# Twelve-head attention of a small vision tower: values kept token-major and passed through DRAM instead of being spread and transposed

## The reference, cut to what matters

```python
qkv = x @ qkv_w.T + qkv_b
q, k, v = (qkv[0], qkv[1], qkv[2])          # B, heads, 17, 16
attn = softmax(einsum('bhqd,bhkd->bhqk', q, k) * scale, axis=-1)
out = einsum('bhqk,bhkd->bhqd', attn, v)
return out @ proj_w.T + proj_b
```

## Time and profile before

| | us |
|---|---|
| median of 3 runs | 935.1 |
| profiled execution, its own time | 934.2 |
| its span | 932.1 |
| stages a0, a2, a3 together | 299.9 |
| PE busy | 854.9 (92% of the span) |
| DVE busy | 447.4 (48%) |
| ACT busy | 387.8 (42%) |
| POOL busy | 186.7 (20%) |

### The profile page before, as it was taken

One profiled execution on the slowest core, in us unless ns is written; L12 is line 12 of the kernel. 1 busy time (PEld: TensorE's weight loads), 2 busy tenths in 40 slices (PEclk: granted clock), 3 DMA queues, 4 the chain that ended last, 5 costly groups with the idle time before them and its releaser, 6 DMA issues. The chain is left out here.

```text
span 932.1 us, 16890 instructions
## 1 busy us (share of the span) xinstructions
PE 854.9 (92%) x6194; PEld 608.5 (65%) x6195; DVE 447.4 (48%) x903; ACT 387.8 (42%) x857; POOL 186.7 (20%) x207
## 2 busy tenths in 40 slices
PE   6899888999998799999989789999999999999997
PEld 5556656677775467777668466765687566666776
DVE  5566676777744412222268666551104566633111
ACT  2366653453542022333243864554151455532332
POOL 0610003444500134445200012220000000002232
PEclk9999999999988899999999999999999999997999
DMA  8000000000004967112150019000000211102111
GB/s 294 1 2 1 1 2 0 1 2 1 1 2 102 256 182 198 46 51 46 39 164 3 0 45 258 6 2 28 1 1 1 56 50 50 52 19 97 43 51 34
DMA packets 30638, 51.07 MB, mean 55 GB/s; under 512 B 3750, under 2 KB 23752, under 8 KB 30572
## 3 DMA queue, kind: packets, MB, share of 16 engines
q1 hardware_dynamic: 22140, 36.09, 14.0%
q0 software_dynamic: 4416, 9.84, 3.8%
q10 hardware_dynamic: 4016, 4.23, 1.4%
HBM read 43.30 MB, written 6.83 MB: 54 GB/s over the span
## 5 line engine op out<-in xcount | busy, mean ns | idle before, releaser
L79 PE MATMUL banks<-con 128*128 128x512 f32 (+1 forms) x206 | 95.1, 572 | 3.0 <-DVEq L2136 1.4
L1846 PE MATMUL banks<-moe_wu,moe_xf 96*128 x256 | 92.1, 505 | 1.6 <-ACT moe_xf L1954 0.8
L634 PE MATMUL banks<-x,a_wqkv 96*96 96x272 f32 x288 | 74.6, 397 | 0.9 <-PEq L457 0.5
L1846 PEld LDWEIGHTS banks<-moe_wu,moe_xf 96*128 96x128 f32 x256 | 47.5, 195 | 31.4 <-issue 4.8
L944 ACT ACTIVATE a_vt<-banks 102x384 f32<-102x384 f32 x96 | 41.9, 488 | 50.4 <-PE banks L710 50.1
L154 ACT ACTIVATE ln_sq<-x 96x544 f32<-96x544 f32 x32 | 21.1, 658 | 93.2 <-DVE x L146 93.2
L634 PEld LDWEIGHTS banks<-x,a_wqkv 96*96 96x96 f32 x288 | 45.4, 164 | 18.2 <-issue 3.2
L79 PEld LDWEIGHTS banks<-con 128*128 128x128 f32 x206 | 38.4, 202 | 25.9 <-issue 22.4
L2151 DVE TENSOR_TENSOR moe_hid<-banks,moe_gs 128x384 f32<-128x384 f32 x32 | 17.9, 558 | 77.6 <-PE banks L1846 77.6
L710 PE MATMUL banks<-con,a_vx 96*102 96x96 f32 x384 | 42.7, 253 | 7.4 <-ACT a_vt L944 6.1
L2008 POOL DMA_INDIRECT moe_xs<-moe_x_rows,moe_taken x32 | 31.2, 974 | 76.1 <-PE banks L1830 54.2
(11 more groups left out here) (409 smaller groups left out, 1772.2 us busy)
## 6 DMA issues: line engine op xcount, KB each, us to landing
moe_wu<-in_moe_up SPq DMA_DIRECT2D x16, 576.0 KB, 8.9
f_w<-in_f_e SPq DMA_DIRECT2D x10, 576.0 KB, 14.6
moe_wd<-in_moe_down SPq DMA_DIRECT2D x16, 288.0 KB, 9.9
patch_px<-in_patches SPq DMA_DIRECT2D x4, 768.0 KB, 9.4
f_wu<-in_f_up SPq DMA_DIRECT2D x4, 582.0 KB
f_wd<-in_f_down SPq DMA_DIRECT2D x4, 576.0 KB
f_x_rows<-f_xtok ACTq DMA_DIRECT2D x4, 384.0 KB, 3.4
a_wqkv<-in_a_wqkv SPq DMA_DIRECT2D x3, 432.0 KB, 8.3
```

The costliest lines, as they stand in the source:

```text
L79: self.nc.tensor.matmul(self.ps[bank][:, 0:width], self.ident, self.con[:, 0:width], start=True, stop=True)
L634: last = nc.tensor.matmul(ps[2 + m][0:HD, 0:CW], wqkv[:, a, j * D + m * HD:j * D + (m + 1) * HD], chunk(x, c)[:, a], start=a == 0, stop=a ...
L1846: last = nc.tensor.matmul(ps[2 + 2 * p + u][:, 0:BW], xf[0:KU[a], p, a], wu[0:KU[a], bass.ds(e, 1), a, u * BW:(u + 1) * BW].rearrange("p e ...
```

## The change

The values are projected token-major: the tokens of `x` are the stationary operand and the value weights the moving one, so that a product gives [128 tokens, 192 features] in PSUM. `values(c)` makes eight such products per chunk (two blocks of 128 tokens and one of 32 for the last 16). ACT moves them to `vtok` in two instructions. SP writes them to a DRAM tensor `v_rows` (two planes of 272 rows of 96 features) with 4 DMAs per chunk, waits for these, and reads them back with 6 DMAs per chunk, one per head of a plane, into `vt`, now with (key, head) in the partitions. Each read writes 18 partitions x 32 pieces of 16 floats (64 bytes); the 18th is a row that no product uses and that makes the number even. `vt` and `vtok` hold two chunks: the read of chunk c waits until `weigh` is done with chunk c-2. Keys, scores and weights change their inner order from (head, key) to (key, head). The loads ahead are issued in four parts, part c after the read of chunk c+1. `spread_values`, `turn_values` and the old `take_values` are gone. In a3 the transposes of the inputs stay, under the name `turn_inputs`. POOL zeroes `vt` first (two memsets).

```diff
@@ ClassWeights
+    PARTS = ((0, 1), (2, 3), (4,), (5,))
...
@@ ExpertWeights
+    def load_part(self, sp, part):
+        self.load(sp, range(part, part + 1))
...
@@ stage_narrow_attention
-        vx = sb("vx", [HD, 2, 2, IC, HH * N])
-        vt = sb("vt", [HH * N, 2, GI, 2, HD])
+        vtok = sb("vtok", [128, 2, 2 * D + HD])
+        vt_rows = sb("vt", [(N + 1) * HH, 2, 2 * IC, HD])
+        vt = vt_rows[0:N * HH].rearrange("p c (a i) d -> p c a i d", a=2)
...
+        v_rows = nc.dram_tensor(name + "_v_rows", (NC, 2 * CW + 1, HD), F32).ap()
...
@@ block.sync
-            for w in ahead:
-                w.load(sp)
+            def write_values(c):
+                rows = v_rows[c, 0:2 * CW].rearrange("(a t) d -> t a d", a=2)
+                for u in range(2):
+                    sp.wait_ge(v_taken, 2 * c + 1)
+                    sp.dma_start(rows[128 * u:128 * (u + 1)], vtok[:, c % 2, u * D:(u + 1) * D].rearrange("p (a d) -> p a d", a=2)).then_inc(v_written, 16)
+                for a in range(2):
+                    sp.wait_ge(v_taken, 2 * c + 2)
+                    sp.dma_start(rows[256:CW, a], vtok[SLOT * (a + 1) - (CW - 256):SLOT * (a + 1), c % 2, 2 * D:2 * D + HD]).then_inc(v_written, 16)
+
+            def read_values(c):
+                sp.wait_ge(v_written, 64 * (c + 1))
+                if c < 2:
+                    sp.wait_ge(vt_zero, c + 1)
+                else:
+                    sp.wait_ge(ctx_ready, GPC * (c - 1))
+                for h in range(HH):
+                    sp.dma_start(vt_rows[h::HH, c % 2, :, h * HW:(h + 1) * HW],
+                                 bass.AP(v_rows.tensor, c * (2 * CW + 1) * HD + h * HW, [[HD, N + 1], [N * HD, 2 * IC], [1, HW]])).then_inc(v_in[c % 2], 16)
+
+            sp.wait_ge(vt_zero, 1)
+            sp.dma_start(v_rows[:, 2 * CW:2 * CW + 1].rearrange("c t d -> t c d"), vt_rows[0:1, 0, 0:NC]).then_inc(v_padded, 16)
+            write_values(0)
+            sp.wait_ge(v_padded, 16)
+            read_values(0)
+            for c in range(NC):
+                if c + 1 < NC:
+                    write_values(c + 1)
+                    read_values(c + 1)
+                for w in ahead:
+                    w.load_part(sp, c)
...
@@ block.tensor
+            def values(c):
+                if c in carried:
+                    pe.wait_ge(before.ready, c + 1)
+                if c >= 1:
+                    pe.wait_ge(v_taken, 2 * c)
+                for u in range(2):
+                    for a in range(2):
+                        tokens = chunk(x, c)[:, a, 128 * u:128 * (u + 1)]
+                        nc.tensor.matmul(v_bank[:, u * D:(u + 1) * D], tokens, wqkv[:, a, 2 * D:3 * D], start=a == 0, stop=a == 1)
...
             def weigh(g):
+                c = g // GPC
                 pe.wait_ge(pt_evicted, g + 1)
-                pe.wait_ge(vt_evicted, (g + 1) * FV)
+                if g % GPC == 0:
+                    pe.wait_ge(v_in[c % 2], 16 * HH * (c // 2 + 1))
...
             for c in range(NC):
                 more = c + 1 < NC
-                turn_values(2 * c)
+                if quantum:
+                    if c == 0:
+                        pe.wait_ge(s_factor, 1)
+                    turn_inputs(2 * c)
+                if c + 2 < NC:
+                    values(c + 2)
...
@@ block.gpsimd
+            for c in range(2):
+                pool.memset(vt_rows[:, c], 0.0).then_inc(vt_zero, 1)
...
@@ block.vector
-            def spread_values(c):
-                for a in range(2):
-                    dve.wait_ge(v_proj, 2 * c + a + 1)
...
```

More of the change, by code:

```diff
@@ L262, in allocate @@
         self.gw_in, self.w_in = self.sem("gw_in"), [self.sem(f"w{i}_in") for i in range(6)]
-    def load(self, sp):
-        sp.dma_start(self.gw[:], self.dram["gw"]).then_inc(self.gw_in, 16)
-        for i in range(6):
+    def load_part(self, sp, part):
+        if part == 0:
+            sp.dma_start(self.gw[:], self.dram["gw"]).then_inc(self.gw_in, 16)
+        for i in self.PARTS[part]:
             w1d = self.dram["p1"] if i == 0 else self.dram["e1"][i - 1]
@@ L280, in allocate, with load_part @@
             self.bg, self.b2 = self.sb("bg", [128, E]), self.sb("b2", [128, E, D])
+    def load_part(self, sp, part):
+        if part == 0:
+            self.load(sp)
     def load(self, sp):
@@ L647, in project_q @@
                     project(c, 0, q_proj, m)
-            def project_v(c, m):
-                pe.wait_ge(qk_evicted, NT * c + 2 + m + 1)
-                project(c, 2, v_proj, m)
+            def values(c):
[7 more added lines that the diff above has]
+                        nc.tensor.matmul(v_bank[:, u * D:(u + 1) * D], tokens, wqkv[:, a, 2 * D:3 * D], start=a == 0, stop=a == 1)
+                for a in range(2):
+                    tokens = chunk(x, c)[:, a, CW - SLOT:CW]
+                    for m in range(2):
+                        last = nc.tensor.matmul(v_bank[SLOT * m:SLOT * (m + 1), 2 * D:2 * D + HD], tokens,
+                                                wqkv[:, a, 2 * D + m * HD:2 * D + (m + 1) * HD], start=a == 0, stop=a == 1)
+                last.then_inc(v_proj, 1)
             def states():
@@ L799, in _ @@
                 pe.wait_ge(wo_in, 32)
+            values(0)
+            if quantum:
                 states()
             project_k(0)
+            values(1)
             for c in carried:
@@ L812, in _ @@
                 head_mean_square(1)
-            for m in range(2):
-                project_v(0, m)
             if rms:
```

162 lines of the change are left out of this document (76 added, 86 removed).

## The result

The kernel after takes 974.6 us (median of 4 runs, 967.66 to 982.5) beside 935.0 us for the kernel before on the same chip: ratio 1.038, 95% interval 1.031 to 1.046, slower. On a second chip the ratio was 1.044 (1.036 to 1.052). The point forecast was 966 us and the measurement lies in its range, but that is luck: of the three large terms one has the wrong sign, the other two are about four times too large, and the largest cost, TensorE's clock, is all but missing from the sum. The profiled execution (982.5 us) lies over 1.5% above the fastest of its kernel, as do those of the runs with the split `f_wu` alone, with all causes mended and with one put back; the last column has one of the second chip, 968.2 us, that does not.

What follows compares the result with a forecast made beforehand. PE's program was taken to bound stages a0, a2 and a3. On the profiled 934.2 us, -16 (a0) + 11 (a2) + 29.8 (a3) + 5 (late rows) + 1.6 (cold clock) = +31 gave 966 us, range 912 to 1005.

Steps and rivals of the forecast that it cites:

- the three large terms: Forecast changes of three stages: a0 -16 us, a2 +11 us, a3 +29.8 us.
- TensorE's clock: Half clock after waits, counted only as 1.6 us in a2 and 1.6 us in the last stage.
- what I took: Reads of values: 28 ns for a 64-byte packet, so 10.8 us for a chunk's read.
- the 39 ns between packets of a short train: Upper bound for a packet in value reads, 15 us a read; as a rival, 1000 us in all, chance 0.2.

Runs made afterwards that it cites:

- the split `f_wu` alone: After, with each f_wu load of 97 partitions issued as 96 partitions and 1: 961.2 us, ratio 1.018.
- all causes mended: After, with value projections moved into gaps, fillers in chunk 2's, a2's norm scaling behind a_ct, f_wu loaded as 96 and 1 partitions: 917.9 us, ratio 0.980.
- one put back: The kernel with all causes mended, but with each f_wu load on one DMA engine again: 946.2 us, ratio 1.009.
- idle products: After, with filler products on TensorE ahead of the second context transposes of a chunk in a0, a2 and a3: 965.35 us, ratio 1.026.

## What to carry to other kernels

Before work is taken from the engine that seems to bind, or moved on it, look at each of its waits: how long it is, and what stands in the gap ahead of it. Taking or moving that away opens the gap, and a gap of 2 us costs more than itself, because TensorE may run at half its clock for many microseconds behind it (17 here). Put real work that can be anywhere (here a projection two chunks ahead) into the gap before judging the change. And try an edit in more than one surrounding: one and the same split gained nothing in before, 13 us in the last stage of after and nothing in its a3, and 28 us, 16 of them in a3, in the mended kernel, depending on what else was late.

## What the runs showed of the hardware

- Reads of 64-byte pieces from DRAM to 18 partitions took 11 to 14 ns of DMA engine time a packet, half or less of what I took and well under the 39 ns between packets of a short train; a read of 3456 of them took 6.7 us, of which its six issues were 4.7.
- Behind a load of 97 partitions SP could hand over the value write only after 16.96 us (after) and 12.64 us (idle products); issued as 96 and 1 partitions it let the last stage's wait fall from 14.77 to 2.59 us.
- Waits of 2.2 to 2.8 us on TensorE, one a chunk in a0, were each followed by the 1.2 GHz level, at which L831 took 3.94 us instead of 2.07, for 7 to 21 us. Of waits of 0.97, 1.60 and 1.60 us in the same place, before the change, only the last was, for 3.3 us.
- A VectorE product of 0.72 us took 3.60 when it started 0.02 us after a GpSimd product, and ended 0.58 us after it.
- Idle products in place of a wait gave a0 a clock of 0.94 where it had 0.77 to 0.79 on the same chip, and took 7 to 9 us off the stage, their own excess over the wait included.
